# A decoder layer on one core: another router and another order ahead of the expert blocks, and block rows turned on VectorE instead of TensorE

## The reference

```python
shared = jax.nn.silu(g) * y @ shared_dw.T            # 704 hidden columns, every token
scores = jax.nn.sigmoid(xf @ gate_w.T)               # 8 experts
_, topk_idx = jax.lax.top_k(scores + gate_bias, 2)
w = jnp.take_along_axis(scores, topk_idx, axis=-1)
w = w / jnp.sum(w, axis=-1, keepdims=True)
for e in range(8):                                   # 352 hidden columns per expert
    g_e, u_e = jnp.split(xf @ up_w[e].T, 2, axis=-1)
    out = out + (jax.nn.silu(g_e) * u_e) @ down_w[e].T * where(topk_idx == e, w, 0)
```

## Time and profile before

| | |
|---|---|
| median of 3 runs | 1074.83 us (1074.69 to 1076.5) |
| the profiled execution's own time | 1065.3 us |
| its span (first to last instruction) | 1063.6 us |
| TensorE clock granted | 0.999 of full speed |
| busy: PE, DVE, ACT, POOL | 96%, 66%, 49%, 50% of the span |
| cross-attention | to about 800 us |
| router and dense unit A | about 804 to 862 us |
| the 21 blocks | about 862 to 1011 us |
| dense unit B, combination, last norm | to 1063.6 us |

### The profile page before, as it was taken

How to read it: one execution, slowest core, us unless ns; L and a number is a source line. 1 busy time by engine, 2 the same in 40 slices (tenths; PEclk the granted TensorE clock), 3 DMA queues, 4 the chain that set the end, 5 groups by cost and what they waited for, 6 DMA issues and landing times.

```text
span 1063.6 us, 20152 instructions
## 1 busy us (share of the span) xinstructions
PE 1021.0 (96%) x7006; PEld 906.5 (85%) x7006; DVE 703.5 (66%) x1452; ACT 523.7 (49%) x1033; POOL 530.0 (50%) x515
## 2 busy tenths in 40 slices
PE   6999888999999999999999999999998999999997
PEld 5866667899999999999999999999886887887786
DVE  4277776777777777777777777767785454554457
ACT  5355545555545555555555455455542345655520
POOL 0156766864633633643643643643572645444543
PEclk9999999999999999999999999999999999999999
DMA  8100104324333233233233233224220769999843
GB/s 285 69 31 2 60 16 136 149 113 147 121 112 116 95 110 115 95 110 115 94 110 115 96 108 115 98 107 152 91 73 1 299 243 376 389 390 378 309 120 108
DMA packets 44697, 153.46 MB, mean 144 GB/s; under 512 B 3704, under 2 KB 3704, under 8 KB 41568
## 3 DMA queue, kind: packets, MB, share of 16 engines
q1 hardware_dynamic: 42400, 145.38, 38.0%
q0 software_dynamic: 2240, 7.34, 2.1%
HBM read 130.04 MB, written 22.66 MB: 144 GB/s over the span
## 4 chain that ended last, share of the span: by engine, by line
PE 74%; DVE 4%; POOL 3%; issue 2%; ACT 2%; POOLq 0%; DVEq 0%; ACTq 0%
PE xa_y_ps L86 6%; PE xa_y_ps L88 6%; PE xa_y_ps L87 5%; PE ex_raw_ey_ps L2078 5%; PE ex_raw_gu_ps L86 4%; PE ex_raw_gu_ps L88 4%; PE ex_raw_gu_ps L87 4%; PE xa_c_ps L1871 4%; PE xa_c_ps L1867 4%; PE xa_c_ps L1866 4%; PE xa_turn_ps L1948 3%; PE xa_turn_ps L1904 3%; PE front_k_ps L86 3%; PE front_k_ps L88 3%; PE front_k_ps L87 3%
## 5 line engine op out<-in xcount | busy, mean ns | idle before, releaser
L1218 POOL TENSOR_TENSOR xa_probs<-xa_probs,xa_inv_sum 112x750 f32<-112x750 f32 x63 | 97.8, 1552 | 75.8 <-DVE xa_inv_sum L1545 75.8
L1494 DVE TENSOR_TENSOR xa_kT_lo<-xa_turn_ps,xa_kT_hi 128x750 fp32r<-128x750 f32 x63 | 59.2, 940 | 99.8 <-ACT xa_kT_hi L1306 99.7
L1203 POOL TENSOR_TENSOR k_ms<-k_ss,sum_eps 125x6 f32<-125x6 f32 x63 | 12.5, 198 | 210.9 <-DVE k_ss L1510 210.9
L1866 PE MATMUL xa_c_ps<-xa_probsT_hi,xa_nat 125*128 125x224 f32 x384 | 92.3, 274 | 2.7 <-ACT xa_probsT_hi L1322 2.7
L1867 PE MATMUL xa_c_ps<-xa_probsT_hi,xa_nat 125*128 125x224 f32 x384 | 92.3, 275 | 0.0
L1206 POOL TENSOR_TENSOR k_inv<-k_ms,neg_half 125x6 f32<-125x6 f32 x63 | 83.4, 1324 | 8.3 <-POOL k_ms L1203 6.6
L1322 ACT CAST xa_probsT_hi<-xa_turn_ps 125x672 fp32r<-125x672 f32 x62 | 44.6, 719 | 87.1 <-PE xa_turn_ps L1948 87.1
L1328 ACT ACTIVATE xa_probs<-xa_scores_ps,xa_bias,xa_q_scale 112x375 f32<-112x375 f32 x126 | 82.6, 662 | 5.7 <-DVE xa_bias L1520 4.4
L1866 PEld LDWEIGHTS xa_c_ps<-xa_probsT_hi,xa_nat 125*128 125x128 f32 x384 | 73.6, 192 | 3.5 <-issue 3.1
L1867 PEld LDWEIGHTS xa_c_ps<-xa_probsT_hi,xa_nat 125*128 125x128 f32 x384 | 73.5, 191 | 0.5
L86 PE MATMUL front_k_ps<-land_xa_wk_hi,land_xa_ctx 128*125 128x256 f32 x252 | 71.4, 283 | 1.4 <-DVE front_k_hat L1537 1.0
(11 more groups left out here) (371 smaller groups left out, 3486.4 us busy)
## 6 DMA issues: line engine op xcount, KB each, us to landing
xa_nat<-ctx_split SPq DMA_DIRECT2D x56, 750.0 KB
ex_raw_raw<-in_w_units SPq DMA_DIRECT2D x15, 1408.0 KB, 7.7
ex_raw_raw<-in_w_units SPq DMA_DIRECT2D x15, 768.0 KB, 7.7
land_ex_raw<-in_w_units SPq DMA_DIRECT2D x8, 1408.0 KB, 7.7
land_ex_raw<-in_w_units SPq DMA_DIRECT2D x8, 768.0 KB, 7.7
ctx_split<-xa_nat SPq DMA_DIRECT2D x8, 750.0 KB
sorted_x<-ex_raw_y_sb SPq DMA_DIRECT2D x7, 768.0 KB, 10.5
ex_raw_x_nat<-sorted_x SPq DMA_DIRECT2D x21, 256.0 KB, 8.1
```

The lines of the kernel that those rows point to most:

```text
L1218: pool.tensor_tensor(probs[0:T, u % 2], probs[0:T, u % 2], inv_sum[0:T, u % 2, :].unsqueeze(2).broadcast_to([T, 2, KV]), ALU.mult).then_in ...
L1494: dve.tensor_tensor(kT_lo[:, :, 0:KV], turn_ps[:, :, 0:KV], kT_hi[:, :, 0:KV].bitcast(F32), ALU.subtract).then_inc(sem["kT_lo_done"], 1)
L1866: pe.matmul(c_view[:, c], nat[0:KT, u % 2, 0, at], probsT_hi[0:KT, :, cols], start=(t == 0), stop=False)
```

## The change

1. The last `join` writes to `turn_ps` (`o_last`), not to `y_ps`, and comes ahead of the wait for the addition of tile 4. The turning of tiles 2 and 3 is moved ahead of that wait too.
2. Tiles 5 and 6 are turned inside `dense_up(0)`, after 18 of its 24 matmuls, not behind it.
3. The gate's high and low halves lie side by side (`gate_hl`), so that `logits_T` takes 16 matmuls, not 24; DVE adds the two halves (`logits_added`). `logits` begins after the first copy.
4. `before`, `every` and `picked` are fp32r; the 7 counting matmuls at the end of `places` become one, and DVE sums over the tiles (one more reduction in `place`).
5. `load_x` issues four transfers, each of 32 partitions with four pieces of 512 bytes, where it issued one of 128 partitions with 2048 bytes. DVE turns the 32x32 pieces into `x_raw` (`turn_block` moves from PE to DVE, at the head of its block), and `xb_hi` and `xb_lo` are made from `x_raw` in SBUF, not from `et_ps` in PSUM. The expert units' rows are laid out to match, on the host.
6. `dense_down(0, 6)` moves from ahead of `block_up(0)` to behind it.

```diff
@@ VectorE
+    def turn_block(j):
+        dve.wait_ge(xs[f"x_{j % 2}_loaded"], 64 * (j // 2 + 1))
+        if j >= 1:
+            dve.wait_ge(xs["xb_lo_done"], j)
+        dve.transpose(x_raw[:].rearrange("p (c b t) -> p b c t", c=DC, t=SQUARE), x_nat[:, j % 2, :].rearrange(
+            "p (b c t) -> p b c t", c=DC, t=SQUARE)).then_inc(xs["xb_turned"], 1)
@@ SyncE, load_x
-    sp.dma_start(x_nat[:, j % 2, :], sorted_x[j * P:(j + 1) * P, :]).then_inc(xs[f"x_{j % 2}_loaded"], 16)
+    rows = sorted_x[j * P:(j + 1) * P, :].rearrange("(b t) d -> t b d", t=SQUARE)
+    for a in range(P // SQUARE):
+        part = x_nat[a * SQUARE:(a + 1) * SQUARE, j % 2, :].rearrange("t (b d) -> t b d", d=P)
+        sp.dma_start(part, rows[:, :, a * P:(a + 1) * P]).then_inc(xs[f"x_{j % 2}_loaded"], 16)
@@ ScalarE, block_x
-    act.copy(xb_hi[:], et_ps[:, 0, :]).then_inc(xs["xb_hi_done"], 1)
+    act.copy(xb_hi[:], x_raw[:]).then_inc(xs["xb_hi_done"], 1)
@@ VectorE, block_low
-    dve.tensor_tensor(xb_lo[:], et_ps[:, 0, :], xb_hi[:].bitcast(F32), ALU.subtract)
+    dve.tensor_tensor(xb_lo[:], x_raw[:], xb_hi[:].bitcast(F32), ALU.subtract)
...
     for j in range(NB):                                   # DVE
+        if j + 1 < NB:
+            turn_block(j + 1)
         up_low(j + 2)
...
-    if j >= 1:
+    if j == 0:
+        add_shared(TILES - 1, 0)
+    else:
         take(j - 1)
@@ VectorE, the loop over add_shared(t, 0), t = 0 to 5
-    block_low(0)
-    add_shared(TILES - 1, 0)
+    if t == TILES - 2:
+        turn_block(0)
+        block_low(0)
@@ TensorE, logits_T
-        mm = three_products(pe, et_ps[0:E, g, 0:HT], gate_hi[:, c, :], gate_lo[:, c, :],
-                            xT_hi[:, c, cols], xT_lo[:, c, cols], c == 0, c == DC - 1)
+        pe.matmul(et_ps[0:2 * E, g, 0:HT], gate_hl[:, c].rearrange("p a e -> p (a e)"), xT_hi[:, c, cols],
+                  start=(c == 0), stop=False)
+        mm = pe.matmul(et_ps[0:E, g, 0:HT], gate_hi[:, c, :], xT_lo[:, c, cols], start=False, stop=(c == DC - 1))
@@ TensorE, places
-    for t in range(TILES):
-        mm = pe.matmul(et_ps[:, 1, 0:E], every[:], picked[:, t, :], start=(t == 0), stop=(t == TILES - 1))
+    pe.matmul(et_ps[:, 1, 0:TILES * E], every[:], picked[:].rearrange("p t e -> p (t e)"), start=True, stop=True)
@@ VectorE, choose
+    dve.wait_ge(xs["logits_ready"], 1)
+    dve.tensor_reduce(score[:], pair, AX_X, ALU.add).then_inc(xs["logits_added"], 1)
@@ TensorE, tail of cross-attention
     output(4, y_ps)
-    added(4)
-    join(N + 2, 0, N // 2 - 1)
+    join(N, 0, N // 2 - 1, o_last)
     turn(pe, 2)
     turn(pe, 3)
+    added(4)
...
-    dense_up(0, 0, up_hi, up_lo)
-    turn(pe, 5)
-    turn(pe, 6)
+    dense_up(0, 0, up_hi, up_lo, last_turns)
...
-    turn_block(0)
-    dense_down(0, TILES - 1, 0)
     for j in range(NB):
         block_up(j)
-        if j + 1 < NB:
-            turn_block(j + 1)
-        if j >= 1:
+        if j == 0:
+            dense_down(0, TILES - 1, 0)
+        else:
             block_down(j - 1)
         turn_hidden(j)
```

More of the change, by code:

```diff
@@ L1397, in probs_high, with output_high @@
                 act.copy(probsT_hi[0:KT], turn_ps[0:KT, :, 0:KT_N * T]).then_inc(sem["probsT_hi_done"], 1)
[L1399 removed]
+            def output_high(j, view):
                 act.wait_ge(sem["o_ready"], j + 1)
[L1402 removed]
+                act.copy(oT_hi[:, :, joined_cols(j)], view).then_inc(sem["oT_hi_done"], 1)
             u = N - 1
@@ L1873, in context_of, with join @@
                 mm.then_inc(sem["c_ready"], 1)
-            def join(s, i, j):
+            def join(s, i, j, view):
                 hold(pe, sem["wv_lo_done"], i, 1, j // HALF + 1)
@@ L1957, in slot @@
                 if j is not None:
-                    join(s, i, j)
+                    join(s, i, j, o_view)
                 u = s - 2
@@ L1999, in places, with dense_up @@
                               picked[:, t, :].unsqueeze(1).broadcast_to([P, later, E]), start=False, stop=(t == TILES - 2))
-                for t in range(TILES):
-                    mm = pe.matmul(et_ps[:, 1, 0:E], every[:], picked[:, t, :], start=(t == 0), stop=(t == TILES - 1))
-                mm.then_inc(xs["places_ready"], 1)
-            def dense_up(k, base, w_hi, w_lo):
+                pe.matmul(et_ps[:, 1, 0:TILES * E], every[:], picked[:].rearrange("p t e -> p (t e)"), start=True,
+                          stop=True).then_inc(xs["places_ready"], 1)
+            def dense_up(k, base, w_hi, w_lo, between=None):
                 g, c = divmod(k, HC)
@@ L2016, in dense_up @@
                                             xT_hi[:, d, cols], xT_lo[:, d, cols], d == 0, d == DC - 1)
+                        if between is not None and (half, d) == (1, 1):
+                            between()
                 mm.then_inc(xs["up_ready"], 1)
@@ L2034, in dense_down @@
                 mm.then_inc(xs["y_ready"], 1)
-            def turn_block(j):
-                pe.wait_ge(xs[f"x_{j % 2}_loaded"], 16 * (j // 2 + 1))
-                if j >= 1:
-                    pe.wait_ge(xs["xb_lo_done"], j)
-                for c in range(DC):
-                    mm = pe.transpose(et_ps[:, 0, c * P:(c + 1) * P], x_nat[:, j % 2, c * P:(c + 1) * P], ident[:])
-                mm.then_inc(xs["xb_turned"], 1)
             def block_up(j):
@@ L2125, in _ @@
             added(2)
-            join(N, 0, N // 2 - 2)
+            join(N, 0, N // 2 - 2, o_view)
             context_of(u - 1, 0)
@@ L2240, with quarters, unit @@
     shared_gw, shared_dw = a["L0_ffn_shared_gw"], a["L0_ffn_shared_dw"]
-    def unit(up, down):
+    def quarters(w):
+        return w.reshape(P // SQUARE, DC, SQUARE, w.shape[1]).transpose(0, 2, 1, 3)
+    def unit(up, down, rows=chunks):
         tail = np.zeros((HC * P - HID, D), down.dtype)
-        return np.concatenate([chunks(up).reshape(P, -1), chunks(np.concatenate([down, tail], axis=0)).reshape(P, -1)], axis=1)
-    units = [unit(a["L0_ffn_up_w"][e].T, a["L0_ffn_down_w"][e].T) for e in range(EXPERTS)]
+        return np.concatenate([rows(up).reshape(P, -1), chunks(np.concatenate([down, tail], axis=0)).reshape(P, -1)], axis=1)
+    units = [unit(a["L0_ffn_up_w"][e].T, a["L0_ffn_down_w"][e].T, quarters) for e in range(EXPERTS)]
     for s in range(SHARED // HID):
```

61 lines of the change are left out of this document (36 added, 25 removed).

## The result

| | median us | runs | profiled execution, us |
|---|---|---|---|
| before | 1075.3 (1074.3 to 1079.3) | 6 | 1065.3 |
| after | 1085.4 (1083.9 to 1088.8) | 6 | 1086.9 |

The ratio is 1.0092, 95% interval 1.0074 to 1.0110: about 10 us slower. 1069.8 and "faster" were forecast, and the range ended at 1079.5.

The account below looks back on a forecast made before the run. In the blocks PE and the DMA were both taken to be at their limit. Front -5.6, way in +0.6 and +0.1 gave -4.9 us; with 5.0 off a 1074.8 us median the forecast was 1069.8, range 1064.0 to 1079.5.

Parts of the forecast that it names:

- Front, -5.6 us: Ahead of the blocks: earlier turnings save 1.6 us, gate product 1.7, small transposes 0.25, counting 2.1; about 5.6 in sum.
- The way in, +0.6 us: From dense work into the blocks: DVE's turning of block 0 puts `block_up(1)` at 868.2, where it was 867.60.
- in front of the blocks the DMA is nearly idle: Ahead of the blocks: the DMA has little to do; PE's waits and small matmuls lie on the chain.
- VectorE's turning, 0.7 us off the path: In each block: DVE's turning of the rows takes 0.7 us, fills an existing wait and is on nobody's path.
- PE with the hold at POOL, a period of 6.9 us: In the blocks, if nothing else binds: `xb_lo` is held until POOL finishes; period 6.9 us, gain 4.7 us in all.
- first rival: Blocks gain too: the quarters cost the DMA nothing, PE with the hold needs 4.7 us less; 1065.1 us, chance 0.21.
- A DMA busy for 0.99 of 7.16 us works 7.1 us per block: In the blocks: the DMA share of 0.99 read as transfer work, so the DMA is at its limit beside PE.
- The quarters' 0.25 us: In each block: four row transfers with 512-byte pieces and 48 more semaphore writes raise DMA work to 7.35 us.
- the main case: Front gains while blocks keep about the old pace, PE's savings becoming waits: 1069.8 us, 1067.3 to 1072.3, chance 0.46.
- The second rival: In the blocks: 32 partitions reached at half rate, DMA work 8.0 us per block, about +7 us, 1081.7; chance 0.22.

Follow-up runs that it names:

- e3_whole_dve: The changed kernel with block rows in one transfer of 128 partitions, exchange between partition groups left out: 1064.3 us, 0.9899 of before.
- f1_front: The kernel before with the change's front part alone; block rows in one transfer, turned by TensorE, old order around block 0: 0.9928 of before.
- e7_whole_early: The changed kernel with block rows in one transfer of 128 partitions and block 0 turned early, after tile 3: 0.9861 of before.

## Why the prediction was wrong

- **Front, -5.6 us: right in the profile.** Each term came within about 0.1 us: 1.57 for 1.6, 1.63 for 1.7, 0.19 for 0.25, 2.2 for 2.1. The runs give the front alone 6.0 to 9.4 us, a little more than that.
- **The way in, +0.6 us: its step left out the clock.** A gap of 2.8 us was in the working (from 859.33, where PE's last matmul ahead of it ends, to about 862.1). What it does to the matmuls behind it was not: they ran at the lower level. Turning block 0 earlier gave back 3.9 and 4.1 us, both of gap and clock. The terms as written also add up to 868.3, not 868.2, and "in front of the blocks the DMA is nearly idle" is true only up to about 830 us: its share is 0.94 from 830 to 840 and 1.01 from 840 to 850 in the same trace. Neither changed the outcome.
- **VectorE's turning, 0.7 us off the path: right.** 0.70 to 0.71 us.
- **PE with the hold at POOL, a period of 6.9 us: right.** 6.89 in two kernels. It was the first rival's mechanism, and the changed kernel could not show it.
- **"A DMA busy for 0.99 of 7.16 us works 7.1 us per block": wrong.** The same bytes went through in 6.54 us. The share of 0.99 was no measure of the time that the transfers need.
- **The quarters' 0.25 us: the step that failed.** Measured are 8.37 - 6.54 = 1.83 us (1.46 by the means of 20). The pieces and all that came with them cost 0.43, somewhat over the 0.25; the partitions, which the main case priced at nothing, cost 1.40. The second rival named the right mechanism and had 0.22. Its number, 8.0 us per block, is near the mean of 7.98 by luck: it took 0.56 us too much for the block of before and 0.74 too little for its neighbours, and the mean has the five faster blocks at the start in it.
- **The sum, by differences of ratios.** The front gives -7.7 us, VectorE's turning with the late block 0 -3.1 (`e3_whole_dve` less `f1_front`, whose intervals overlap), the quarters +20.7. Differences along a chain of kernels add up to the whole of +9.9 by themselves, so this splits the change and tests nothing. A test is the quarters' share by periods: 20 x (7.98 - 6.89) = 21.8 us, beside the 20.7.

The version to keep is `f1_front`: 0.9928 of before and 0.984 of after. VectorE's turning is worth 0.0067, 7 us, beyond it (`e7_whole_early`), but that kernel leaves out the exchange between partition groups, and no load tried here brings it the right rows without the loss.

## What to carry to other kernels

A DMA share near 1 in a stretch that another engine bounds is no measure of the DMA's work: thin out that engine's work once, and read the period that is left. Before a transfer to all partitions is cut up, ask which partitions and how many DMA engines each part reaches; the number of parts and their small pieces cost nothing that showed behind TensorE here, 32 or 64 neighbours did, and the load that fits 4 engines was far worse. Look at single periods and not only at their mean: here it had the five faster blocks at the start in it. And take a second profile of a kernel whose profiled execution differs from its median, before a difference of stages is explained.

## What the runs showed of the hardware

- Two transfers of 64 neighbouring partitions cost nearly as much per block (7.69 us) as four of 32 (7.83); four of every fourth partition left it at 7.18.
- 256 KB per block in quarters of 32 neighbours lengthened a block that the transfers bound from 6.54 to 7.94 us, and the rate fell from 419 to 345 GB/s (900 to 980 us).
- At one place of dense unit A, ScalarE starts a silu late (by 5.4 us in the second profile of before: its product ends at about 848.7, the silu starts at 854.10) or VectorE an addition (by 3 us). TensorE idles 3.5 to 6.0 us for it in 17 of 20 profiles and 0.61 in three. The trace names no cause, and none was tested.
